# Result stores of 22 of 32 tiles cut in two by rows, in an attention and expert-lookup kernel

## The reference, cut to what matters

```python
x = x + xattn(layernorm(x), ctx_1024, ...)
# the expert layer, on the layernorm of the new x:
q = normalised over all tokens(x @ w_q)              # 2 x 8 heads x 128
sx, ix = top_k(sim[0], 8); sy, iy = top_k(sim[1], 8)   # sim: q times 128 keys
scores, pk = top_k(sx[..., :, None] + sy[..., None, :], 8)
indices = ix * 128 + iy                                # at pk
wd = down_embed[indices]; wu = up_embed[indices]
h = softmax(scores) * gelu(einsum('bnd,bnhkd->bnhk', x, wd))
out = einsum('bnhk,bnhkd->bnd', h, wu)
x = x + out
```

## Time and profile before

| | us |
|---|---|
| median of three runs | 3224.49 |
| lowest, highest run | 3223.93, 3227.54 |
| span of the profiled execution, first to last instruction | 3223.2 |
| TensorE busy in it | 2869.0 (89%) |
| VectorE busy | 2408.6 (75%) |
| GpSimd busy | 2141.0 (66%) |
| ScalarE busy | 1821.2 (57%) |
| DMA time in the chain that ended last | 56% |
| moved by DMA | 1133.07 MB |

### The profile page before, as it was taken

The page is one execution under the profiler, slowest core; times in us unless marked ns, Lnnn a source line. Parts: engine busy times, 40 slices in busy tenths (PEclk is TensorE's granted clock), DMA queues, the critical chain, the costliest instruction groups (busy, mean ns, idle before and its releaser), DMA issues.

```text
span 3223.2 us, 36101 instructions
## 1 busy us (share of the span) xinstructions
PE 2869.0 (89%) x10310; PEld 1376.2 (43%) x10310; DVE 2408.6 (75%) x5229; ACT 1821.2 (57%) x5592; POOL 2141.0 (66%) x2224
## 2 busy tenths in 40 slices
PE   8999999998888888888898888888888888888877
PEld 6777767433333333333333333333333333333322
DVE  5888716977777777777777777777777777777765
ACT  3566503665565555655556555555556555565555
POOL 1555513777777777777777777777777777777773
PEclk9999999999999999999999999999999999999999
DMA  6222103999999999999999999999999999999996
GB/s 228 78 70 76 38 30 138 412 412 411 412 412 411 412 412 412 411 412 412 412 411 412 412 412 412 412 411 410 411 411 406 411 409 412 404 412 403 412 411 254
DMA packets 324861, 1133.07 MB, mean 352 GB/s; under 512 B 36331, under 2 KB 36971, under 8 KB 324024
## 3 DMA queue, kind: packets, MB, share of 16 engines
q0 software_dynamic: 294912, 1073.87, 83.2%
q1 hardware_dynamic: 29088, 56.41, 4.9%
q10 hardware_dynamic: 664, 0.50, 0.1%
HBM read 1113.87 MB, written 16.78 MB: 351 GB/s over the span
## 4 chain that ended last, share of the span: by engine, by line
DMA 56%; PE 13%; issue 9%; DVE 4%; POOL 2%; ACT 0%; POOLq 0%; ACTq 0%; DVEq 0%
DMA rows<-in_table,expert_idx 51%; PE banks L1382 9%; DMA expert_more_rows<-in_table,expert_idx 5%; POOL rows L793 2%; PE banks L1371 2%; PE banks L1306 1%; DVE expert_top_i L901 1%; DVE expert_diag L992 1%; DVE expert_top_s L893 1%; DVE rows L978 1%; PE banks L1318 0%; DVE expert_coef L984 0%; PE banks L1347 0%; DVE expert_best_i L924 0%; POOL expert_more_rows L793 0%
## 5 line engine op out<-in xcount | busy, mean ns | idle before, releaser
L793 POOL DMA_INDIRECT rows<-in_table,expert_idx x1824 | 1725.1, 946 | 655.1 <-DMA rows<-in_table,expert_idx 512.0
L1382 PE MATMUL banks<-rows,expert_diag 128*128 128x512 f32 x3640 | 1714.5, 616 | 289.0 <-DVE expert_diag L992 288.5
L1194 ACT ACTIVATE rows<-rows 128x512 f32<-128x512 f32 x1820 | 1121.8, 617 | 939.0 <-DVE expert_coef L984 936.9
L978 DVE TENSOR_TENSOR rows<-rows,banks 128x2048 f32<-128x2048 f32 x455 | 1040.9, 2288 | 551.3 <-DMA rows<-in_table,expert_idx 551.3
L1382 PEld LDWEIGHTS banks<-rows,expert_diag 128*128 128x128 f32 x3640 | 687.9, 195 | 1266.9 <-issue 751.8
L1371 PE MATMUL banks<-amat,expert_xnT 128*128 128x512 f32 x992 | 465.6, 593 | 3.7 <-ACT banks L1185 3.0
L992 DVE TENSOR_TENSOR expert_diag<-banks,expert_coef 128x512 f32<-128x512 f32 x511 | 348.0, 681 | 0.7
L1194 ACT ACTIVATION_READ_ACCUMULATOR rows<-rows 128x1 f32 x1820 | 339.3, 186 | 0.0
L1371 PEld LDWEIGHTS banks<-amat,expert_xnT 128*128 128x128 f32 x992 | 188.5, 190 | 240.5 <-issue 228.7
L793 POOL DMA_INDIRECT expert_more_rows<-in_table,expert_idx x224 | 212.4, 948 | 85.2 <-DMA expert_more_rows<-in_table,expert_idx 47.9
L1382 PE MATMUL banks<-expert_more_rows,expert_diag 128*128 128x512 f32 x448 | 216.5, 629 | 38.9 <-DVE expert_diag L992 38.9
(11 more groups left out here) (133 smaller groups left out, 2099.7 us busy)
## 6 DMA issues: line engine op xcount, KB each, us to landing
rows<-in_table,expert_idx POOLq DMA_INDIRECT x1824, 14.8
attention_xT_t<-in_x_T SPq DMA_DIRECT2D x32, 256.0 KB, 3.1
attention_x_t<-in_x SPq DMA_DIRECT2D x32, 256.0 KB, 3.0
x_dram<-rows SPq DMA_DIRECT2D x32, 256.0 KB, 2.0
expert_x_t<-x_dram SPq DMA_DIRECT2D x32, 256.0 KB, 6.1
out_y<-expert_x_t SPq DMA_DIRECT2D x32, 256.0 KB, 6.1
rows<-in_w_q SPq DMA_DIRECT2D x4, 1024.0 KB, 6.2
rows<-in_w_qT SPq DMA_DIRECT2D x4, 1024.0 KB, 8.4
```

The source lines that it names most:

```text
L793: gather = pool.indirect_dma_start(four(n)[:, k, :], None, table[:, :], bass.IndirectOffsetOnAxis(ap=idx[:, t % 2, at:at + 1], axis=0), en ...
L978: return dve.tensor_tensor(down, down, xn_ps[:, par, :].unsqueeze(1).to_broadcast([P, HALF, D]), ALU.mult)
L1194: ins = act.activation(down, down, ACT.Copy, accum_out=hid[:, j % RING, k:k + 1])
L1382: mm = pe.matmul(out_ps[:, par, :], diag[:, j % RING, k, :], four(t * HALVES + j)[:, k, D:2 * D], start=(j == 0 and k == 0), stop=(j == HA ...
```

## The change

A table `STORE_SPLIT` gives for each tile a number of rows, 128 for tiles 0 to 7, 20 and 21. For the other 22 tiles it is less than 128, and the store is made in two DMAs, the first with that many rows and the second with the rest, both on the same semaphore. `stored` counts what the semaphore will reach, so that each wait asks for all DMAs of all stores so far. The waits need these counts as constants, so the hardware loop becomes 28 turns written out at build time. The loads, the order of loads and stores and the bytes are as before.

```diff
+STORE_SPLIT = [P] * 8 + [120, 126, 117, 108, 121, 100, 119, 114, 125, 124, 123, 122] + [P] * 2 + [120] * 10
+
+def parts(first):
+    return [slice(0, P)] if first == P else [slice(0, first), slice(first, P)]
...
+            stored = [0, 0]
+
             def store(t, par, half):
+                x2 = x2_t[:, bass.ts(ring(t, par, half), D)]
                 wait(sp, "y_done", t + 1)
-                sp.dma_start(out_v[t], x2_t[:, bass.ts(ring(t, par, half), D)])\
-                  .then_inc(y_out[par], 16)
+                for rows_of in parts(STORE_SPLIT[t]):
+                    sp.dma_start(out_v[t][rows_of, :], x2[rows_of, :]).then_inc(y_out[par], 16)
+                    stored[par] += 16
...
-            with sp.Fori(0, NT // 2 - 2) as half:
-                for par in range(2):
-                    t = half * 2 + par
-                    if par == 0:
-                        store_t, store_half = t + 1, half
-                    else:
-                        store_t, store_half = t + 1, half + 1
-
-                    sp.wait_ge(y_out[par], (half + 1) * 16)
-                    load(t + 4, par, half + 2)
-                    store(store_t, 1 - par, store_half)
+            for t in range(NT - 4):
+                par, half = t % 2, t // 2
+                sp.wait_ge(y_out[par], stored[par])
+                load(t + 4, par, half + 2)
+                store(t + 1, 1 - par, (t + 1) // 2)
             for t in range(NT - 3, NT):
                 store(t, t % 2, t // 2)
             for par in range(2):
-                sp.wait_ge(y_out[par], 16 * (NT // 2))
+                sp.wait_ge(y_out[par], stored[par])
```

## The result

The changed kernel took 3231.16 us (median of 15 runs, 3229.2 to 3233.8), the kernel before 3224.23 us on the same chips (15 runs, 3223.04 to 3227.54). The ratio is 1.0019, with a 95% interval of 1.0011 to 1.0026. I had predicted 3212.0 us, 12.5 us faster. The sign was wrong, and the time lies above my range (3208.5 to 3230). By the ratio the loss is 6.1 us, by the two medians 6.9 us. The profiled execution has a span of 3228.1 us against 3223.2 us, so 4.9 us of the loss are in the two traces compared here.

A forecast was written before the change was run, and what follows sets the result against it. The prediction took one slow DMA engine, pacing the gathers, to bound the expert stage. Terms of -12.9, +0.3 and +0.1 us summed to -12.5 us, giving 3212.0 us from 3224.5, with a range of 3208.5 to 3230 us.

The forecast's parts named there:

- The bound: Expert stage: runs at the pace of the gathers, its length the work of one slow DMA engine, first to last.
- Step 1: Split stores: equal shares over as many engines as divide the rows; +178 rows on the first engine to -176 on the sixteenth.
- Step 2: Price of a 2 KB row on the slow engine: 76 ns; 22 shares less on the sixteenth save 13.4 to 14.0 us.
- The weak step: Which DMA engine is slow: the sixteenth, given 0.52 as a judgement not worked out from a row.
- the term of -12.9 us: Gain on the slow engine, taken as the sixteenth, capped where the next slowest engine takes over: -12.9 us.
- rival (b): Slow engine is the fourth to fifteenth: +5.6 to -6.7 us, most within 0.2%, around 3222 us; chance 0.22.
- Step 3: End of the gathers: the next slowest engine is 12.9 us ahead, so the gain stops at 12.9 us.
- Step 4: Rows moved to the first two engines: 178 more each, 13.5 us, costed at nothing because they end some 20 us earlier.
- rival (c): Slow engine the sixteenth, next slowest among the first three takes over: gain 0 to 4 us, 3222 us; chance 0.06.
- Step 5: Later landing of split stores, delaying SyncE's next load: tile 19 lands in 16 or 33 us; price 0 to 2, taken 0.
- Step 6: SyncE's own work: 22 more DMAs hidden except the last, 0.3 us; written-out loop's instruction fetches 0.1 us.
- Rival (a): Slow engine is one of the first three, gaining 116 to 178 rows: +8.8 to +13.5 us, 3233 to 3238 us; chance 0.16.

The follow-up runs named there:

- e19_120: All 22 split tiles stored in 120 and 8 rows, against the kernel before at 3224.76 us: 3226.87 us, ratio 1.0007.
- e7_four_again: Only tiles 12 to 15 split, in 124 and 4 rows, against the kernel before at 3224.98 us: 3229.98 us, ratio 1.0016.
- e20_first: Tiles 12 to 15 stored in 61, 64 and 3 rows, against the kernel before: 3223.84 us, ratio 0.9998.
- e1_loop_only: SyncE's loop written out, no store split, against the kernel before at 3568.03 us on a slower chip: 3567.13 us, ratio 0.9998.

## Why the prediction was wrong

**The bound** was right. One engine paces the gathers, and work put on it is paid in full: the loss at `finish` follows its rows tile by tile. The slow engine ends 27.3 us after the last gather was asked for before (3183.6 to 3210.9), and 27.0 us after it in the changed kernel (3188.0 to 3215.0): GpSimd asks as fast as that engine delivers, so a later engine moves all that follows. (Two readings were loose: the two links of the earlier trace rows are 56 of 69 us, four fifths and not nearly all, and the slices of the earlier trace rows go down to 403 GB/s.)

**Step 1, equal shares over as many engines as divide the rows** held. 178 rows for the next slowest (13.6 us against 13.5), the fall of the loss at tiles 18 and 19, and the split in three and in four all need exactly this rule, counted from the first engine. The rule of the Trainium skill that I set beside it, "DMA: Bandwidth & Descriptors", section "Why a DMA increments its semaphore by 16 and not by 1", agrees with these numbers.

**Step 2, 76 ns a row**, was a little high: 66 ns by the fit here, 71 and 72 ns in `e19_120`, `e7_four_again` and `e20_first`.

**The weak step failed, and it carried the sign.** I gave the sixteenth engine 0.52 on a judgement that no row supported. It is the fourth, which gets 74 rows more instead of 176 less: the term of -12.9 us was about +5 us. What I leaned on for the judgement, the Trainium skill, "DMA: Bandwidth & Descriptors", section "Latency and other measured facts" (engines 7 and 15, counted from 0, are usually slower), doesn't hold for this kernel: counted like that, here they are engines 3 and 1, and what they fetch is the likely cause. My list had the right figure for it, +74 rows, +5.6 us, inside rival (b), but (b) mixed places from +5.6 to -6.7 us and was read as "no change"; the measured +6.1 us by the ratio lies at its edge. Even odds over sixteen places would have given a loss of more than 2 us to five of them and a gain of more than 6 us to two. An honest range from the rows would have run to 3238 us.

**Step 3**, the cap by the next slowest, never came to bear, but its lead of 12.9 us was real: it was used up to 3.5 us here, and to about 2 us by the three-engine split.

**Step 4 failed too**, without an effect on the time. I cost the rows on the first two engines at nothing, since both "end some 20 us before the slow engine". The second is the next slowest, 12.9 us ahead, and got 13.6 us. So even with the sixteenth engine as the slow one the gain of 12.9 us would have been gone: rival (c), to which I gave 0.06.

**Step 5** was right in its cheap form. The store of tile 19 is the longest wait of SyncE for a landing:

```profile
SPq L744 <- DMA out_y<-expert_x_t: 16.9, 1, 16.9
```

I had 16 us if a row of the store waits for one gathered row, 33 us if longer. Nothing was late.

**Step 6**: the second DMA at the end cost 0.5 us, against 0.3. The written-out loop cost nothing that could be measured.

**Rival (a)** had the right mechanism, a loss by rows on a slow engine near the front, and the wrong place; by its bounds (first three) it would have been 9 to 13 us.

## What to carry to other kernels

When a stage is paced by DMA, look at how it ends: windows of 2 us after the last issue show how many engines are still running and by how much each trails. If one runs alone, its number has to be measured before work is moved, with two small splits that differ for one engine, not guessed. The parts of a store whose rows don't divide by 16 went to the low-numbered engines here, and the two latest engines were among them. Where gathers paced the kernel, 2044 more waits on VectorE cost 13.1 us, though VectorE had idle time to spare. And before a chip is called slower at something, look at windows of a few us: a mean of 352 GB/s was made of stretches at 421 and at 194.

## What the runs showed of the hardware

- The 16 DMA engines of a core are not equally loaded by instruction fetches. 2044 more instructions on VectorE, with 1 us idle in each step of 5.2 us, cost 13.1 us through one DMA engine, most simply the fourth; the same number on ScalarE cost nothing, but some 10 us of the lead of another, most simply the second. A fetch of 128 instructions came to 0.6 to 0.8 us of that engine.
- A DMA of 61 rows, a prime number, loaded neither the second nor the fourth engine (`e20_first`), as it would if it went over the first alone; one of 122 goes over two, by the 13.6 us of the next slowest engine. In tile 19 it took 16.9 us to land among the gathers, where 128 rows over sixteen take 6.1 us.
- The chips differ: on some the same kernel took 3543 to 3568 us, at 352 to 369 GB/s over 100 us (`e1_loop_only`) instead of 412, and all engines stopped together at the end. On these, moving work between engines changed nothing beyond 0.1%, and some 2040 more instructions cost 0.3 to 0.4% on either engine. The gathers reached 421 GB/s in between; VectorE stood still for up to 18.9 us at once, and what stops it is open.
